# Sixteen DRAM copies of each rstd row, and broadcasts that read each copy for 4 partitions

## The reference, cut to what matters

```python
x = x + conv3x3_shift(_ln_c(x))          # _ln_c: (x - mean) / sqrt(var + 1e-6) over the 64 channels
t = _to_tokens(x)                         # the 64 channels of a pixel are one token
Wx = _ln_t(t) @ W.T                       # _ln_t: the same with 1e-5; first part of the _L0_ffn
```

## Time and profile before

| | |
|---|---|
| median of 3 runs | 1811.79 us (1809.84 to 1813.19) |
| the profiled execution | 1808.75 us, its span 1806.9 us |
| busy share of the span | PE 79%, DVE 77%, ACT 67%, POOL 77% |
| moved by DMA | 429.77 MB, mean 238 GB/s |
| broadcasts of rstd, first stage | 128 DMAs of 512 KB |
| writes of rstd, first and third stage | 256 DMAs of 8 KB |

### The profile page before, as it was taken

One profiled execution on the slowest core, in us unless ns is written; L12 is line 12 of the kernel. 1 busy time (PEld: TensorE's weight loads), 2 busy tenths in 40 slices (PEclk: granted clock), 3 DMA queues, 4 the chain that ended last, 5 costly groups with the idle time before them and its releaser, 6 DMA issues. The chain is left out here.

```text
span 1806.9 us, 23730 instructions
## 1 busy us (share of the span) xinstructions
PE 1426.4 (79%) x5369; PEld 588.6 (33%) x5369; DVE 1382.4 (77%) x2395; ACT 1219.3 (67%) x2321; POOL 1396.7 (77%) x1029
## 2 busy tenths in 40 slices
PE   3889999999999964999944789999999999816100
PEld 1233333333333322666622433333333333205100
DVE  1899999999999953999936469999999999941000
ACT  2678877888788753999933588888898898610000
POOL 2899999999999930398884099999999999801575
PEclk8999999999999997999986799999999999955555
DMA  4579999999999868599986158988988887660011
GB/s 132 156 213 284 279 290 267 284 283 281 288 271 288 231 211 338 209 421 425 421 340 242 45 166 262 295 288 266 298 285 274 287 281 227 205 171 7 1 2 2
DMA packets 111403, 429.77 MB, mean 238 GB/s; under 512 B 44672, under 2 KB 47648, under 8 KB 66208
## 3 DMA queue, kind: packets, MB, share of 16 engines
q1 hardware_dynamic: 91376, 423.77, 72.8%
q10 hardware_dynamic: 16432, 4.29, 1.4%
q0 software_dynamic: 3456, 0.19, 0.2%
HBM read 257.89 MB, written 170.01 MB: 237 GB/s over the span
## 5 line engine op out<-in xcount | busy, mean ns | idle before, releaser
L599 DVE SCALAR_TENSOR_TENSOR pst<-xn,kk,pst 128x512 f32<-128x512 f32 x448 | 336.0, 750 | 8.5 <-PE pst L431 2.3
L431 PE MATMUL pst<-xn,taps 128*128 128x512 f32 x512 | 244.9, 600 | 45.6 <-DVE acc L599 45.6
L541 POOL TENSOR_TENSOR x_and_products<-tap_products,x_and_products 128x512 f32<-128x512 f32 x192 | 245.0, 1276 | 30.1 <-ACT tap_products L509 2.7
L1508 POOL TENSOR_SCALAR exp_q<-exp_q 128x512 f32<-128x512 f32 x128 | 189.5, 1480 | 71.9 <-ACT exp_q L1459 71.9
L925 DVE SCALAR_TENSOR_TENSOR pss<-region,bn,pss 128x256 f32<-128x256 f32 x432 | 195.5, 489 | 45.5 <-PE pss L837 45.0
L509 ACT ACTIVATE tap_products<-xn,kk 128x512 f32<-128x512 f32 x320 | 213.6, 709 | 19.5 <-POOL x_and_products L541 16.1
L1503 POOL TENSOR_TENSOR sq_norm<-x_ring 128x512 f32<-128x512 f32 x128 | 188.6, 1474 | 6.0 <-DVE x_ring L1555 2.0
L541 POOL TENSOR_TENSOR x_and_products<-tap_products,x_ring 128x512 f32<-128x512 f32 x128 | 163.2, 1275 | 23.7 <-ACT tap_products L509 23.5
L548 POOL TENSOR_TENSOR x_ring<-acc,x_and_products 128x512 f32<-128x512 f32 x128 | 163.6, 1278 | 9.9 <-DVE acc L599 8.7
L874 POOL TENSOR_TENSOR x_block<-x_block,region 128x2048 f32<-128x2048 f32 x28 | 155.7, 5559 | 17.1 <-DMA x_block<-x_scratch 14.3
L1515 POOL TENSOR_TENSOR q_z<-q_map,z_inv 128x512 f32<-128x512 f32 x128 | 164.1, 1282 | 0.0
(11 more groups left out here) (237 smaller groups left out, 2834.2 us busy)
## 6 DMA issues: line engine op xcount, KB each, us to landing
rstd_wide<-rstd_scratch SPq DMA_DIRECT2D x128, 512.0 KB, 11.1
x_ring<-in_x SPq DMA_DIRECT2D x32, 1024.0 KB, 7.9
x_scratch<-x_ring SPq DMA_DIRECT2D x32, 1024.0 KB, 5.0
xl_scratch<-wx SPq DMA_DIRECT2D x32, 1024.0 KB, 15.4
region<-xl_scratch SPq DMA_DIRECT2D x32, 1024.0 KB, 12.3
x_ring<-x_scratch SPq DMA_DIRECT2D x32, 1024.0 KB, 5.7
rstd_of_channels<-rstd_scratch SPq DMA_DIRECT2D x64, 512.0 KB, 7.7
out<-x_ring SPq DMA_DIRECT2D x32, 1024.0 KB, 6.6
```

The lines of the kernel that those rows point to most:

```text
L431: m = pe.matmul(wide(pst[g % 2]), taps[:, n * P:(n + 1) * P], tap_rows(g, t), start=(n == 0), stop=(n == len(mine) - 1))
L541: pool.tensor_tensor(xr[:, g % XR, :], prod[:, q % NP, :, :].rearrange("p r w -> p (r w)"), xr[:, g % XR, :] if n else x_tile(g), ALU.add) ...
L599: dve.scalar_tensor_tensor(out=out, in0=tap_rows(g, t), scalar=kk[:, t:t + 1], in1=wide(pst[g % 2]), op0=ALU.mult, op1=ALU.add).then_inc(a ...
L1508: pool.tensor_scalar(e, e, 1.0, None, ALU.min).then_inc(clipped, 1)
```

## The change

The DRAM scratch gets one slot per round with all 32 rows (norm, batch, 8 equal rows) and a second copy of each ("twin"). `rstd_to_dram` now writes, for each of the 4 tiles and each of 2 twins, 32 partitions of 2 KB: 64 KB per DMA, eight DMAs in each round, whether it has one norm or two. Each row of 2048 values thus stands 16 times in DRAM (8 equal rows x 2 twins), one behind the other. A broadcast reads these 16 copies, each for 4 partitions. Its bytes, destinations and number stay.

```diff
-            rstd_d = [dram(f"rstd_scratch{l}", (NBLK, B, BLOCK)) for l in range(2)]
...
+            rstd_d = dram("rstd_scratch", (ROUNDS, 32, 2, BLOCK))
+
...
             def rstd_written(n):
 
-                return rstd_out[n % 2], sum(16 * B * len(norms_in(m)) for m in range(n % 2, n + 1, 2))
+                return rstd_out[n % 2], 16 * 2 * TPB * (n // 2 + 1)
...
                 def rstd_to_dram(n):
                     sp.wait_ge(rstd_ready, n + 1)
-                    for l, k in norms_in(n):
-                        for b in range(B):
-                            sp.dma_start(rstd_d[l][k, b, :].rearrange("(j n) -> j n", n=TILE),
-                                         rstd[16 * l + 8 * b:P:32, n % 2, :]).then_inc(rstd_out[n % 2], 16)
+                    for j in range(TPB):
+                        for twin in range(2):
+                            sp.dma_start(rstd_d[n, :, twin, cols_of(j)],
+                                         rstd[32 * j:32 * j + 32, n % 2, :]).then_inc(rstd_out[n % 2], 16)
...
                     for b in range(B):
+                        rows = rstd_d[round_of(l, k), 16 * l + 8 * b:16 * l + 8 * b + 8, :, :].rearrange("r w n -> (r w) n")
                         sp.dma_start(rb[l][b * C:(b + 1) * C, k % 2, :],
-                                     rstd_d[l][k, b, :].partition_broadcast(C)).then_inc(rb_loaded[l][k % 2], 16)
+                                     rows.unsqueeze(1).to_broadcast([16, C // 16, BLOCK])).then_inc(rb_loaded[l][k % 2], 16)
```

## The result

The changed kernel takes 1833.43 us (median of 4 runs, 1828.93 to 1841.81) beside 1811.07 for the kernel before in the same comparison (4 runs). The ratio is 1.0129 [1.0103, 1.0156]: 22 us slower. The forecast was 1847 in a range of 1814 to 1862. The sign and the range held; the size was too large by 14 us.

A forecast was written before the change was run, and what follows sets the result against it. DVE and DMA were both taken as nearly full in the first stage, with DMA becoming the bound. Steady rounds +31, broadcast wait -2, start +3, end +3.5 gave +35.5 us: 1844, or 1847 against the median; range 1814 to 1862.

The forecast's parts named there:

- Broadcasts stay as they are: First stage: 64 destination partitions, not the shared row, limit broadcasts to 216 GB/s, so 9.7 us a round stays.
- Rival 1: The shared row was the limit: broadcasts fall to 4.9 us a round, about +19 us, 1831 us; chance 0.10.
- Writes, issue: SP's queue: eight writes a round take 3.4 to 4.2 us, delaying everything behind them by 1.3 to 2.1 us.
- The loop: Rstd, write issue, load of x, ACT's square, next rstd: 17.6 us a round becomes 18.9 to 19.7.
- Writes, bytes: 491 KB more a round costs 1.9 us of DMA, which becomes the bound: +1.3 us in 24 rounds, +31 us.
- Broadcast wait: DVE's 2.3 us of slack before needing broadcast rows is used up by the first late rounds: -2 us, once.
- Start: First round: six more writes delay the first norm by 3.2 us, 2.3 with the cheaper issue; counted as +3 us.
- End: Last two rounds: extra issues and bytes on SP delay stores of u that DVE awaits: +3.5 us, between 0 and 6.
- Sum: Whole kernel: 31 - 2 + 3 + 3.5 = 35.5 us over the profiled execution, 1844; 1847 against the median.
- Rival 3: No change: added writes fit beside other packets, loop 18.9, steady part gains 0 to 2 us; 1814 us; chance 0.11.
- Rival 2: Faster: broadcasts at 4.9 us and write issue under 0.41 us leave the steady part unmoved: -7 us, 1805; chance 0.07.

The follow-up runs named there:

- e11_full_width: Kernel before, with one 1 MB broadcast per norm reading a single row of ones 128 times into all 128 partitions, without multiplying by rstd: 1803.49 us, ratio 0.9952.
- e2_one_row: Changed kernel with its eight writes, but each broadcast reads one row 64 times as before the change: 1841.77 us, ratio 1.0186.
- e6_wide: Changed kernel with one 1 MB broadcast per norm into 128 partitions from 16 rows, four 64 KB writes, no second copy: 1813.95 us, ratio 1.0016.
- e4_small_writes: Kernel before, with each 8 KB write issued twice, the second into a copy that nothing reads: 1843.58 us, ratio 1.0191.
- e10_small_behind: e4_small_writes with the four second writes moved behind the load of x on SP's queue: 1811.27 us, ratio 1.0002 to the kernel before.
- e3_four_writes: Changed kernel with both copies of a tile in one 128 KB DMA, four issues and the same bytes: 1815.08 us, ratio 1.0031.
- e5: Changed kernel with the store of x1 and the load of x ahead of the writes on SP's queue: 1870.93 us, ratio 1.0334.
- e7: e6_wide with the store of x1 and the load of x ahead of the writes on SP's queue: 1842.38 us, ratio 1.0175 to the kernel before.
- e8: Kernel before, with the store of x1 and the load of x ahead of the writes on SP's queue: 1838.08 us, ratio 1.0142.

## Why the prediction was right, and where not

**Broadcasts stay as they are: right.** 226 GB/s where 216 was kept. The expert weights pointed to the destination, though weakly: other loads (L1739, L1740, L1743) were under way in that stretch too. e11_full_width bears it out for one row, 419 GB/s at full width. The Trainium skill's rule (SBUF — State Buffer, "Door 1: The DMA port swizzle"), with its estimate of 218 GB/s for a half, agrees with 216 to 229 here into 64 partitions from one queue. By that rule alone the copies are worth nothing; the runs show some 8 us once DMA is full (e2_one_row beside the changed kernel). Nor does the width alone account for e6_wide, which fills all 128 partitions at 229. Rival 1 was therefore true in a small way, some 4% of the rate instead of a doubling, and the text kept 9.7 us a round for it without a term between.

**Writes, issue: right in mechanism and size.** Eight writes take 3.6 to 3.9 us, inside 3.4 to 4.2, each 0.424 us by the median, as the nearer row had it. The load comes 1.3 us later in the rounds shown (4.21 instead of 2.90) and 1.5 on average, inside 1.3 to 2.1. The loop was forecast at 18.9 to 19.7; 18.89 was read in one round and 19.4 on average. e4_small_writes and e10_small_behind show that it is the place ahead of the load that costs.

**Writes, bytes: the step that failed.** The prediction took 1.9 us for them, put DMA's work at 20.1 us a round (19.4 to 20.5) and concluded "DMA becomes the bound: +1.3 us a round". Measured is +0.55, and ACT's wait for the load closes the round. e3_four_writes moves the same bytes in rounds of 19.06 us, so DMA's work is no more than that, below the prediction's lower bound. Two terms were too large. The broadcasts: not quite 9.7 us, since 230 for 221 takes 0.4 us off. The bytes: with 18.2 - 0.4 and a round of 19.4 x 0.99 = 19.2, the writes' share of DMA is an estimate of some 1.4 us, nearer to the 1.15 of 426 GB/s than to the 2.3 of 216. The rate of the writes by themselves was not measured. What the bytes do cost comes through a load that lands later in the same loop (9.04 us after its issue in e3_four_writes, 8.27 before).

Behind that stands an error of method. Two candidates for the bound, the loop (18.9 to 19.7) and DMA (19.4 to 20.5), overlapped; the sum took the later one as if it were sure. What was measured, 19.4, lies in the upper half of the loop's range: 18.9 by the cheaper issue, some 0.1 because that issue comes out a little dearer on average, and 0.4 because the load takes 8.44 us on average from its issue to the square in these rounds, where the prediction counted 8.02, the median landing of the whole span and 0.12. That the total still lies in the range is in part luck: the bound that the prediction chose is not the one that held, and the two lay close together.

**Broadcast wait: not paid as put.** The -2 us assumed that late rounds would first eat DVE's slack against the broadcasts. DVE's waits for them in the steady part stayed small (4.3 us from 130 to 600 us); what was late was the load.

**Start: right.** The first norm comes 2.7 us later (forecast 3, and 2.3 with the cheaper issue). Up to round 6 it is 4.6: the rounds without the store of u, which the prediction called covered by DVE, lose 1.9; ACT's waits for loads up to there go from 8.4 us in 2 to 13.8 us in 6, as in the loop.

**End: right.** 4.3 us against 3.5, in the stores of u: DVE waits 9.64 and 5.63 us for two of them.

**Sum.** Forecast 35.5 above the profiled execution, measured 24.2. The steady part explains it: 31 - 2 against 12.7; the small terms were each within 2 us or so of their values, and 2.7 us behind the stage had no term.

Rival 3 had the issue cost right and the loop 0.5 us too short (18.9), and its time of 1814 is nearly that of e3_four_writes, not of this change. Rival 2 named the point that decides, an issue under 0.41 us, and 0.424 is above it; but even with broadcasts twice as fast and no added issue, e11_full_width gains 7 us and no more, the sum of that rival.

## What to carry to other kernels

A DMA added to an in-order queue delays whatever stands behind it, so look for the transfer behind it that closes a loop back to the queue's own next trigger: here four issues ahead of a load cost 33 us, and behind it nothing. Small writes whose landing the queue itself waits for did better ahead of large transfers than behind them (e5, e7 and e8 beside the same kernels in the old order). Before adding copies to speed up a broadcast, ask how many partitions it fills at a time; here, with one source row, the full width was worth up to a factor of two (419 beside 216 GB/s), and 16 source rows at half the width some 4%.

## What the hardware showed that was not expected

- One DRAM row read 128 times runs at 419 GB/s into 128 partitions in the first broadcast of a round and at 335 in the second (e11_full_width), 16 rows read 8 times each into the same 128 partitions at 229 (e6_wide). Both fill all partitions. Why e6_wide is so much slower stays open: the runs don't show how its packets are dealt to engines and partitions.
- Two halves from two queues reach 266 GB/s together, from one queue 216.
- A smaller write can be dearer to issue: a DMA of 8 KB out of 4 partitions holds SP for 0.50 us by the median, one of 64 KB out of 32 partitions for 0.424 us:

```profile
L351 SPq DMA_DIRECT2D rstd_scratch<-rstd x288: 307/424/1410, 32.2 to 683.0; - x144
```

- A DMA share near 1.00 is no proof that DMA sets the time: e6_wide has 0.99 with rounds of 18.74 us, which are DVE's.

**Still open** besides that: the 2.7 us in the unchanged stages, which the spread between runs covers, and what the changed kernel would take with its second copy written behind the load. None of the versions that compute the reference beat the kernel before.
